# Sinkhorn rounds: expert sums in four strips of output rows, masked by batch and spread by one product

## The reference

```
x = x + 0.5 * ffn(layernorm(x));  x = x + mixer(layernorm(x));  x = x + 0.5 * ffn(layernorm(x))
gate_logits = x @ gate_w                      # per batch: 2048 tokens x 8 experts
t = log(clip(gate_logits, 1e-6))
repeat 8 times:
    t = t - logsumexp(t, over tokens)         # each expert of a batch sums to 1
    t = t - logsumexp(t, over experts)        # each token sums to 1
gates = exp(t)
```

## Time and profile before

| | us |
|---|---|
| median of 3 runs (lowest, highest) | 3552.97 (3552.73, 3556.18) |
| the profiled execution's own time | 3554.35 |
| its span, first to last instruction | 3552.7 |
| busy: DVE | 3121.4 (88%) |
| busy: PE, PEld | 2683.9 (76%), 1514.4 (43%) |
| busy: ACT, POOL | 2067.9 (58%), 1323.4 (37%) |

### The profile page before, as it was taken

How to read it: one execution, slowest core, us unless ns; L and a number is a source line. 1 busy time by engine, 2 the same in 40 slices (tenths; PEclk the granted TensorE clock), 3 DMA queues, 4 the chain that set the end, 5 groups by cost and what they waited for, 6 DMA issues and landing times. The chain is left out here.

```text
span 3552.7 us, 29642 instructions
## 1 busy us (share of the span) xinstructions
PE 2683.9 (76%) x9556; PEld 1514.4 (43%) x9556; DVE 3121.4 (88%) x2760; ACT 2067.9 (58%) x2171; POOL 1323.4 (37%) x897
## 2 busy tenths in 40 slices
PE   6503788899789889978988997898789777407663
PEld 4402343355346335534633553463344245406542
DVE  7897579999999999999999999999999977898432
ACT  6101467876877787687778768777876734003110
POOL 0003254446245444624544462454011110006777
PEclk8556799999899999989999998999899888557876
DMA  8103278688778868877886887787667669102222
GB/s 335 63 0 100 77 176 182 148 174 179 160 170 168 183 148 174 180 159 170 170 183 147 174 180 160 170 171 176 122 139 145 130 118 364 40 0 80 91 92 81
DMA packets 124568, 521.98 MB, mean 147 GB/s; under 512 B 19753, under 2 KB 55271, under 8 KB 80416
## 3 DMA queue, kind: packets, MB, share of 16 engines
q0 software_dynamic: 76704, 397.27, 53.6%
q1 hardware_dynamic: 47744, 123.29, 9.6%
HBM read 137.94 MB, written 102.77 MB: 68 GB/s over the span
## 5 line engine op out<-in xcount | busy, mean ns | idle before, releaser
L1253 DVE TENSOR_TENSOR_SCAN state<-state,drive 128x2048 f32<-128x2048 f32 x512 | 2224.0, 4404 | 51.5 <-ACT state L1459 51.3
L1459 ACT ACTIVATE state<-delta,neg_a 128x2048 f32<-128x2048 f32 x512 | 1018.3, 2004 | 216.4 <-DMA delta<-xc 85.5
L1710 PE MATMUL ps_states<-state,ident 128*128 128x512 f32 x1792 | 854.5, 622 | 76.4 <-DMA state<-state 62.0
L1134 POOL DMA_DIRECT2D state<-state x255 | 234.0, 918 | 1309.3 <-DVE state L1253 1290.2
L1612 PE MATMUL ps_proj<-x1t,w_in 128*128 128x512 f32 x1024 | 514.7, 649 | 85.9 <-ACT xc L1408 31.0
L1710 PEld LDWEIGHTS ps_states<-state,ident 128*128 128x128 f32 x1792 | 349.2, 201 | 479.7 <-issue 385.1
L1628 PE MATMUL ps_proj<-conv_in,tap 128*128 128x512 f32 x1024 | 488.9, 629 | 55.2 <-ACT conv_in L1372 34.6
L1063 POOL DMA_INDIRECT picked<-normed_rows,slot_now x112 | 353.5, 3156 | 100.5 <-PE ps_rows L1593 55.8
L1612 PEld LDWEIGHTS ps_proj<-x1t,w_in 128*128 128x128 f32 x1024 | 207.3, 207 | 370.6 <-issue 281.5
L1079 POOL DMA_INDIRECT x<-routed_rows,row_now x112 | 336.3, 3003 | 34.6 <-issue 34.6
L1628 PEld LDWEIGHTS ps_proj<-conv_in,tap 128*128 128x128 f32 x1024 | 204.4, 202 | 321.5 <-issue 280.9
(11 more groups left out here) (321 smaller groups left out, 3173.8 us busy)
## 6 DMA issues: line engine op xcount, KB each, us to landing
state<-state POOLq DMA_DIRECT2D x255, 1024.0 KB, 7.5
delta<-xc POOLq DMA_DIRECT2D x24, 1024.0 KB, 11.8
normed_rows<-rows_in SPq DMA_DIRECT2D x8, 2048.0 KB, 7.8
x_rows<-x SPq DMA_DIRECT2D x16, 1024.0 KB, 8.2
rows_in<-in_x SPq DMA_DIRECT2D x7, 2048.0 KB, 13.1
expert<-in_experts SPq DMA_DIRECT2D x56, 256.0 KB, 4.8
routed_rows<-routed SPq DMA_DIRECT2D x112, 128.0 KB, 3.2
x<-in_x POOLq DMA_DIRECT2D x14, 1024.0 KB, 8.9
```

Of the source, the lines that this page charges most:

```text
L1134: nc.gpsimd.dma_start(out=state[held(q)][:], in_=state[held(q - 1)][:], accum_op=ALU.add).then_inc(pair_landed(b, q // 2)[0], 16)
L1253: nc.vector.tensor_tensor_scan(state[held(q)][:], state[held(q)][:], drive[j % 2][:], 0.0, ALU.mult, ALU.add).then_inc(state_ready, 1)
L1459: nc.scalar.activation(state[held(q)][:], delta[j % 2][:], ACT.Exp, scale=g.neg_a[:, j, n:n + 1]).then_inc(decay_ready, 1)
L1710: mm = nc.tensor.matmul(ps_sum[c][:], g.ident[:], state[held(q)][:, c * CH:(c + 1) * CH], start=(opening and n == 1), stop=(n == N - 1))
```

## The change

The sums of a half are now made in four strips of output rows of the same bank: group z goes to rows 32 * (z % 4) and the three after them, so four products follow each other in four strips, and each strip adds up four groups. The other rows of `ps_sum`, now 128 x 32, hold zeros, for which VectorE clears both banks ahead of the loop; the first sums wait for that. The mask `own` is 128 x 32, with ones in the same four rows of each strip. VectorE first multiplies the sums by the mask (`keep_own`, into `own_sum`). One product with ones of 128 x 128 then adds up strips and rows and spreads the sums over all partitions. VectorE inverts that (128 x 32) and multiplies probs by it out of SBUF. In VectorE's queue the order of a step is: reciprocal and product of this half, mask of the other half, sum over experts and token reciprocal of this half.

```
--- before.py
+++ after.py
@@ -185,18 +185,19 @@
     token_sum = sb("token_sum", [P, 2, Q, 2, H, HB])
     scaled_p = sb("scaled_probs", [P, 2, Q, 2, H, HB, E])
     gates = sb("gates", [P, 2, Q, 2, H, HB, E])
-    own = sb("own_batch", [HB, HB, E])
-    expert_scale = [sb(f"expert_scale{h}", [HB, HB, E]) for h in range(H)]
-    inverse = [sb(f"inverse{h}", [HB, HB * E]) for h in range(H)]
-    inverse_done = [sem(f"inverse_done{h}") for h in range(H)]
-    ps_sum = [ps_logit[h][0:HB, 0:HB * E] for h in range(H)]
+    STRIP = P // Q
+    own = sb("own_batch", [P, HB, E])
+    own_sum = [sb(f"own_sum{h}", [P, HB * E]) for h in range(H)]
+    expert_scale = [sb(f"expert_scale{h}", [P, HB * E]) for h in range(H)]
+    ps_sum = [ps_logit[h][:, 0:HB * E] for h in range(H)]
+    sums_cleared = sem("sums_cleared")
     ps_scale = [ps_turn[4 + h][:, 0:HB * E] for h in range(H)]
     ps_rows = ps_turn[0:4]
     own_made, probs_ready, sums_ready, gates_done, rows_turned = (
         sem(n) for n in ("own_made", "probs_ready", "sums_ready", "gates_done", "rows_turned"))
-    r_done, sums_done, expert_done, scale_spread, token_scaled = (
-        [sem(f"{n}{h}") for h in range(H)] for n in ("token_scale_done", "expert_sums_done", "expert_scale_done",
-                                                     "scale_spread", "token_scaled"))
+    r_done, sums_done, own_done, sum_spread, expert_done, token_scaled = (
+        [sem(f"{n}{h}") for h in range(H)] for n in ("token_scale_done", "expert_sums_done", "own_sum_done",
+                                                     "sum_spread", "expert_scale_done", "token_scaled"))
     eps_set, summed, wide_set, stats_done, moments_done, std_done, rstd_done, shift_done = (
         sem(n) for n in ("eps_set", "gate_summed", "wide_gate_set", "stats_done", "moments_done", "std_done", "rstd_done",
                          "shift_done"))
@@ -228,9 +229,10 @@
     @block.gpsimd
     def _(pool):
         nc.gpsimd.memset(own[:], 0.0).then_inc(own_made, 1)
-        pool.wait_ge(own_made, 1)
-        nc.gpsimd.affine_select(out=own[:], in_=own[:], compare_op=ALU.not_equal, fill=1.0,
-                                base=0, pattern=[[1, HB], [0, E]], channel_multiplier=-1).then_inc(own_made, 1)
+        for strip in range(Q):
+            pool.wait_ge(own_made, strip + 1)
+            nc.gpsimd.affine_select(out=own[:], in_=own[:], compare_op=ALU.not_equal, fill=1.0, base=strip * STRIP,
+                                    pattern=[[1, HB], [0, E]], channel_multiplier=-1).then_inc(own_made, 1)
 
     @block.sync
     def _(sp):
@@ -338,37 +340,39 @@
         dve.wait_ge(scaled, 2)
         flat = probs[:].rearrange("p o q k h b e -> p (o q k h b e)")
         nc.vector.tensor_scalar(flat, flat, CLIP, None, ALU.max).then_inc(probs_ready, 1)
+        dve.wait_ge(rows_copied, 2)
+        for h in range(H):
+            nc.vector.memset(ps_sum[h], 0.0).then_inc(sums_cleared, 1)
+
+        def keep_own(h, i):
+            dve.wait_ge(sums_done[h], i + 1)
+            nc.vector.tensor_tensor(own_sum[h][:], ps_sum[h], own[:].rearrange("p b e -> p (b e)"), ALU.mult
+                                    ).then_inc(own_done[h], 1)
 
         def scale_of_experts(h, i):
-            dve.wait_ge(sums_done[h], i + 1)
-            nc.vector.reciprocal(inverse[h][:], ps_sum[h]).then_inc(inverse_done[h], 1)
-            dve.wait_ge(inverse_done[h], i + 1)
-            nc.vector.tensor_tensor(expert_scale[h][:].rearrange("q b e -> q (b e)"), inverse[h][:],
-                                    own[:].rearrange("q b e -> q (b e)"), ALU.mult).then_inc(expert_done[h], 1)
-
-        def sums_of_tokens(h, i):
-            dve.wait_ge(scale_spread[h], i + 1)
+            dve.wait_ge(sum_spread[h], i + 1)
+            nc.vector.reciprocal(expert_scale[h][:], ps_scale[h]).then_inc(expert_done[h], 1)
+            dve.wait_ge(expert_done[h], i + 1)
             nc.vector.tensor_tensor(of_probs(scaled_p, h), of_probs(probs, h),
-                                    ps_scale[h].unsqueeze(1).to_broadcast([P, Z, HB * E]), ALU.mult
+                                    expert_scale[h][:].unsqueeze(1).to_broadcast([P, Z, HB * E]), ALU.mult
                                     ).then_inc(token_scaled[h], 1)
+
+        def scale_of_tokens(h, i):
             dve.wait_ge(token_scaled[h], i + 1)
             nc.vector.tensor_reduce(of_tokens(token_sum, h), of_probs(scaled_p, h).rearrange("p z (b e) -> p z b e", e=E),
                                     AX.X, ALU.add).then_inc(sums_ready, 1)
-
-        def scale_of_tokens(h, i):
             dve.wait_ge(sums_ready, H * i + h + 1)
             nc.vector.reciprocal(of_tokens(r, h), of_tokens(token_sum, h)).then_inc(r_done[h], 1)
 
-        dve.wait_ge(probs_ready, 1)
-        dve.wait_ge(own_made, 2)
-        scale_of_experts(0, 0)
+        dve.wait_ge(own_made, Q + 1)
+        keep_own(0, 0)
         for i in range(ITERS):
             for h in range(H):
-                sums_of_tokens(h, i)
+                scale_of_experts(h, i)
                 if h + 1 < H:
-                    scale_of_experts(h + 1, i)
+                    keep_own(h + 1, i)
                 elif i + 1 < ITERS:
-                    scale_of_experts(0, i + 1)
+                    keep_own(0, i + 1)
                 scale_of_tokens(h, i)
         for h in range(H):
             dve.wait_ge(r_done[h], ITERS + 1)
@@ -470,20 +474,21 @@
         def sums_of_experts(h, i):
             pe.wait_ge(r_done[h], i + 1)
             for z in range(Z):
-                mm = nc.tensor.matmul(ps_sum[h], of_tokens(r, h)[:, z, :], of_probs(probs, h)[:, z, :],
-                                      start=(z == 0), stop=(z == Z - 1))
+                strip = z % Q * STRIP
+                mm = nc.tensor.matmul(ps_sum[h][strip:strip + HB, :], of_tokens(r, h)[:, z, :], of_probs(probs, h)[:, z, :],
+                                      start=(z < Q), stop=(z >= Z - Q))
             mm.then_inc(sums_done[h], 1)
 
-        def spread_scale(h, i):
-            pe.wait_ge(expert_done[h], i + 1)
-            nc.tensor.matmul(ps_scale[h], g.ones[0:HB, :], expert_scale[h][:].rearrange("q b e -> q (b e)"),
-                             start=True, stop=True).then_inc(scale_spread[h], 1)
+        def spread_sums(h, i):
+            pe.wait_ge(own_done[h], i + 1)
+            nc.tensor.matmul(ps_scale[h], g.ones[:], own_sum[h][:], start=True, stop=True).then_inc(sum_spread[h], 1)
 
         pe.wait_ge(probs_ready, 1)
+        pe.wait_ge(sums_cleared, H)
         sums_of_experts(0, 0)
         for i in range(ITERS):
             for h in range(H):
-                spread_scale(h, i)
+                spread_sums(h, i)
                 if h + 1 < H:
                     sums_of_experts(h + 1, i)
                 elif i + 1 < ITERS:
```

## The result

Measured in 6 runs each on the same chips: 3524.89 us (3519.56 to 3529.48) after, 3551.61 us (3549.95 to 3556.18) before; ratio 0.9921, 95% interval 0.9911 to 0.9932. That is 26.7 us less, where 25.6 were forecast. The profiled execution took 3522.61 us, its span 3521.1 us.

What follows compares the result with a forecast made beforehand. Bound: TensorE and VectorE waiting for each other in the Sinkhorn loops, TensorE's 1.87 us sums the largest term of a 3.07 us step. Gaining 12.8 us a stage, 25.6 in both, gives 3527.3 us; range 3520 to 3542.

Steps and rivals of the forecast that it cites:

- The strips: TensorE's sums in the Sinkhorn loop: four strips stream side by side, 0.65 us in place of 1.87; full overlap, chance 0.63.
- L445's rows: Logits products in strips before the change, starting some 0.013 us apart; taken as the model for the sums' 0.65 us.
- L736's pitch: Rival for the sums: pair issue at 0.030 us is the floor, sums 1.17 us, 3537.8 us; chance 0.24 with half overlap.
- VectorE's step: One half-batch step of the Sinkhorn loop on VectorE, summed from start-to-start times: 2.30 us, against 3.08 before.
- The spread with 128 rows: TensorE's product spreading the sums in the loop: still 0.63 us with 128 rows in place of 4, slack 0.40.
- The start: Ahead of the first sums: two PSUM memsets, at most 0.25 us, move TensorE's start from 99.87 to about 100.05.
- The new bound: In the loop, VectorE has no wait left and sets the 2.30 us step; sums wait for the token reciprocal.
- The slack of 0.19 in the sums: In the loop, sums can be read at 2.11 us, the next mask is due at 2.30: 0.19 us to spare.
- The stages: Sinkhorn loops of both routings: each gains 12.8 us, 25.6 us in both.
- The end: Whole kernel: time falls by the loops' 25.6 us to 3527.3; later stages shift it only by +-3 us.
- The slower rival: Rival for the sums: short products do not overlap, sums stay 1.87 us, step 3.33, 3560.2 us; chance 0.04.

Runs made afterwards that it cites:

- One strip: Changed kernel with all sixteen products of a half in the first strip, order, mask and spread kept: 3558.87 us, 1.0022 of the kernel before.
- two strips: Changed kernel with the products of the sums going to two strips in turn instead of four: 3531.88 us, 0.9948 of the kernel before.

## Why the prediction was right

- *The strips.* Forecast 0.65 us for the sums, measured 0.61. L445's rows, at the same clock, were the right neighbour, and L736's pitch was no floor: 31 starts in 0.61 - 0.24 us are 0.012 us apart. One strip, two strips and four (1.87, 1.02, 0.61 us) show that it is the strips. The Trainium skill's figures in "TensorE: Matmul & The Clock Gate" (Wait — 56ns, not 53.3ns?: never below about 25 ns from start to start) and in "TensorEngine Tiling (Array Packing)" (Instruction Overhead: about 60 cycles each) do not hold across strips here.
- *VectorE's step.* Forecast 2.30, measured 2.24 to 2.25. Of its terms, product to mask (0.61), mask to sum over experts (0.11) and sum to token reciprocal (0.72) were right within 0.01. Reciprocal to product was 0.33, not 0.38: behind another reciprocal, as in every step, the reciprocal takes 0.30; only the first one of a loop, where VectorE had stood idle, took 0.36, about the 0.35 that I had taken. The token reciprocal was 0.02 longer.
- *The spread with 128 rows.* 0.64 us against 0.63, as taken. It hides: 102.54 + 0.64 = 103.18, wanted at 103.61.
- *The start.* Clip to first sums 0.23 us against 0.06: 0.17 more, forecast 0.18.
- *The new bound.* VectorE without a wait, the sums late by their start: both as forecast. The slack of 0.19 in the sums comes out near that with two strips (sums 0.41 longer, step 0.25 longer: 0.16 were free).
- *The stages.* Gain 12.8 forecast for each; 13.6 and 11.7 measured. The sum, 25.3 against 25.6, is that close by luck, since two errors cancel: steps faster by 0.05, and the 1.8 us that the second loop lost to gaps, which the prediction did not see, because the loop before had none under the same traffic.
- *The end.* 25.6 forecast, 26.7 measured by the medians. The likeliest value of 3527.3 stood on a median of before of 3552.97, which was 1.4 lower over six runs. The 1.4 us by which the medians gained more than the loops is within the spread of the runs.
- *The slower rival* was priced well: one strip 3558.9, forecast 3560.2.

## What to carry to other kernels

Where two engines hand a small thing back and forth, write the step as a ring of start-to-start times from the trace and ask, for each edit, which engine closes it next. Products with few columns of weights can go to different strips of output rows in turn; how much this gives is read from any line of the kernel that does it already. A shorter term pays in full only if the latency behind it is covered too: here the new arrangement of the other engine's work, its order above all, was worth 5 of 13.5 us a loop, and cost 3.7 without the shorter term.

## What the runs showed of the hardware

- Short products in four strips start 0.012 us apart on average at half clock (four at 0.007, then 0.053 to the next four), also where both records of a product go to the same strip; filled in blocks they overlap only in part (1.17 us).
- A float32 product on GpSimd has some 0.69 us of fixed cost, then 1.06 ns a column (32 to 96 columns on 128 partitions).
- The length of a reciprocal on VectorE hardly grew with the partitions: after an idle time 0.36 us for 128x32 and 0.35 for 4x32. What ran before it counted for more: 128x32 took 0.30 us right behind another reciprocal.
- TensorE stopped in the middle of a row of ready products for 0.5 to 1.1 us, at places 256 instructions apart, while the DMA queues were full (share 0.99) or just as that traffic ended, and nowhere in the loop once it was moved. The cause is argued, not shown.
